# A Mamba block and an expert feed-forward layer on one core: statistics of x moved to ScalarE, one product of B and u moved from GpSimd to VectorE

## What is computed

```
x = x + mamba(layernorm(x))          # and inside it: rmsnorm, x @ W_in -> xs, res
    xs = silu(conv4(xs) + conv_b)    # 512 channels
    dt = softplus((xs @ W_x)[:, :512] @ W_dt);  B, C = 16 columns each of xs @ W_x
    h_t = exp(-exp(A_log) * dt_t) * h_(t-1) + dt_t * B_t * xs_t    # 512 channels x 16 states
    y_t = sum over the 16 states of h_t * C_t;   out = (y * silu(res)) @ W_out + residual
x = x + (silu(n @ w1[e]) * (n @ w3[e])) @ w2[e],  n = layernorm(x)   # expert e for tokens 512 e .. 512 e + 511
```

## Time and profile before

| | |
|---|---|
| median of three runs | 983.43 us |
| the profiled execution, its own time | 983.61 us |
| its span, first to last instruction | 981.8 us |
| TensorE matmul busy | 915.7 us (93%) |
| VectorE busy | 899.1 us (92%) |
| GpSimd busy | 891.0 us (91%) |
| ScalarE busy | 733.2 us (75%) |
| granted TensorE clock, mean | 0.979 |

### The profile page before, as it was taken

The page is one execution under the profiler, slowest core; times in us unless marked ns, Lnnn a source line. Parts: engine busy times, 40 slices in busy tenths (PEclk is TensorE's granted clock), DMA queues, the critical chain, the costliest instruction groups (busy, mean ns, idle before and its releaser), DMA issues.

```text
span 981.8 us, 13018 instructions
## 1 busy us (share of the span) xinstructions
PE 915.7 (93%) x4172; PEld 598.0 (61%) x4172; DVE 899.1 (92%) x966; ACT 733.2 (75%) x1305; POOL 891.0 (91%) x425
## 2 busy tenths in 40 slices
PE   6989989999999999999999999999999997869898
PEld 4555455655766566755756557755766566745765
DVE  5889899899999999999999999999999989999951
ACT  4577877988779878888779888888779785567630
POOL 1498899999999999999999999999999999999920
PEclk9998999999999999999999999999999999679899
DMA  5580144012742049021561038220480027200110
GB/s 175 212 308 22 43 185 204 4 65 65 268 186 67 2 148 353 18 68 59 212 247 43 25 103 326 89 68 21 176 320 16 31 99 284 92 21 4 59 50 21
DMA packets 43476, 116.82 MB, mean 119 GB/s; under 512 B 8592, under 2 KB 27024, under 8 KB 34192
## 3 DMA queue, kind: packets, MB, share of 16 engines
q1 hardware_dynamic: 41552, 115.94, 32.0%
q10 hardware_dynamic: 1856, 0.04, 0.1%
HBM read 110.21 MB, written 5.77 MB: 118 GB/s over the span
## 4 chain that ended last, share of the span: by engine, by line
PE 44%; DVE 20%; issue 14%; ACT 11%; POOL 10%; DMA 1%; DVEq 0%; POOLq 0%; SPq 0%; ACTq 0%
PE gbank L1095 18%; DVE ring L658 13%; PE gbank L1109 12%; PE ybank L1158 9%; POOL hc L516 7%; DVE ring L643 4%; ACT ebank L787 2%; POOL ring L502 2%; ACT hb L1022 2%; ACT sres L872 1%; DVE hb L738 1%; PE gbank L1103 1%; ACT L1027 1%; ACT L1020 1%; DMA hb<-in_L_attn_W_x_dram 1%
## 5 line engine op out<-in xcount | busy, mean ns | idle before, releaser
L658 DVE TENSOR_TENSOR_SCAN ring<-ebank,state,ring 128x512 f32<-128x512 f32 x512 | 623.2, 1268 | 31.1 <-ACT ebank L787 24.1
L516 POOL TENSOR_TENSOR hc<-ring,c_all 128x1024 f32<-128x1024 f32 x255 | 598.5, 2368 | 12.8 <-PE ybank L1158 6.9
L787 ACT ACTIVATE ebank<-dt_,a_neg 128x512 f32<-128x512 f32 x512 | 348.0, 688 | 149.6 <-DVE ring L658 145.8
L1158 PEld LDWEIGHTS ybank<-ident,hc 128*128 128x128 f32 x2048 | 239.1, 144 | 107.3 <-issue 54.9
L1158 PE MATMUL ybank<-ident,hc 128*128 128x128 f32 x2048 | 266.0, 279 | 33.2 <-POOL hc L516 19.2
L502 POOL TENSOR_TENSOR ring<-b_all,u 128x1024 f32<-128x1024 f32 x109 | 258.1, 2368 | 9.9 <-DVE taken L607 9.5
L643 DVE TENSOR_TENSOR ring<-b_all,ubank 128x1024 f32<-128x1024 f32 x145 | 173.5, 1196 | 0.0
L1095 PE MATMUL gbank<-xT,w 128*128 128x512 f32 x320 | 147.9, 597 | 9.8 <-DVE hb L738 8.5
L1095 PE MATMUL gbank<-xT,w_a 128*128 128x512 f32 x256 | 119.7, 604 | 8.0 <-DVE dt_ L632 4.4
L1095 PEld LDWEIGHTS gbank<-xT,w 128*128 128x128 f32 x320 | 57.3, 190 | 76.5 <-issue 56.7
L1095 PE MATMUL gbank<-xs,w_a 128*128 128x512 f32 x224 | 100.8, 593 | 0.7 <-ACT sres L805 0.7
(11 more groups left out here) (146 smaller groups left out, 749.4 us busy)
## 6 DMA issues: line engine op xcount, KB each, us to landing
b_all<-bc_kept SPq DMA_DIRECT2D x32, 1024.0 KB, 6.6
c_all<-bc_kept SPq DMA_DIRECT2D x32, 1024.0 KB, 8.4
w<-in_L_ffn_w_dram SPq DMA_DIRECT2D x16, 640.0 KB, 4.9
w_a<-in_L_attn_W_in_dram SPq DMA_DIRECT2D x7, 1024.0 KB, 5.0
w_a<-wc_kept SPq DMA_DIRECT2D x7, 1024.0 KB, 4.9
w2s<-in_L_ffn_w_dram SPq DMA_DIRECT2D x8, 640.0 KB, 9.3
xin<-in_L_attn_x_dram SPq DMA_DIRECT2D x9, 512.0 KB, 3.6
x<-in_L_attn_x_dram SPq DMA_DIRECT2D x7, 512.0 KB, 6.5
```

Source lines behind the costliest of these rows:

```text
L516: ch_ok.by(e.tensor_tensor(hc[:, q % HC, :, :], ring[:, q % RING, :, :], c_all[:, n:n + NG, :], ALU.mult))
L658: h_ok.by(e.tensor_tensor_scan(row, ebank[j % 2][:, :], row, initial=state[:, q, n:n + 1], op0=ALU.mult, op1=ALU.add))
L787: e_ok.by(e.activation(ebank[j % 2][:, :], dt_[:, d, :], ACT.Exp, scale=a_neg[:, d, k:k + 1]))
L1158: last = e.matmul(ybank[:, cols(b)], hc[:, q % HC, n, cols(b)], ident[:, :], is_transpose=True, start=(k == 0 and n == 0 and b == 0), stop ...
```

## The change

- The statistics of x for chunks 2 to 7 leave VectorE. ScalarE makes them instead: `x_sums` are four Copy activations of 128x256 whose accumulator output is the sum of a row, `x_mean` is one small activation, and `x_squares` are four Square activations with the negated mean as bias, again with accumulators. Their full results go to blocks 0 and 1 of `u` and are never used. `rooted` divides by 256 within its scale, and loses one small Copy.
- In iterations 1 to 5 they stand behind tiles 17, 21, 22 and 23 on ScalarE, and `rooted` moves from tile 22 to 26. GpSimd's `front` moves from tile 21 to 26, behind u's first block. GpSimd's products u of blocks 0 and 1 wait for the statistics, since these write there.
- The product of B and u of tile 21 goes from GpSimd to VectorE, where it stands behind `hidden` and `gated(1)`; `gated(1)` moves behind tile 20's `hidden` jobs.
- `residual(0, 1)` behind tile 5 becomes `residual(0)` behind tile 4 and `residual(1)` behind tile 5.
- Iteration 0 has its own places (tiles 23 to 26).

The diff, cut to its core:

```diff
-    POOL_BU = (1, 4, 7, 10, 11, 14, 17, 18, 21, 22, 23, 24, 27, 29)
+    POOL_BU = (1, 4, 7, 10, 11, 14, 17, 18, 22, 23, 24, 27, 29)
+    BEHIND = 21
+        sums = Event("sums", NT)
 # GpSimd, u_of
                     xs_ok.wait(e, c)
+                    if d < 2 and 1 <= c < E - 1:
+                        stats.wait(e, c + 1)
                     ub_ok.wait(e, c - 1, d + 1)
-            table = [(4, "scan", u_of(ND - 1)), (10, "back", back), (21, "next", front), (24, "front", u_of(0)),
+            table = [(4, "scan", u_of(ND - 1)), (10, "back", back), (24, "front", u_of(0)), (26, "next", front),
-            table0 = [..., (23, "next", front),
+            table0 = [..., (26, "next", front),
 # VectorE
+            def bu_behind(c, i):
+                bu(c, BEHIND)
-                if q + 1 < Q and q + 1 in dve_bu(c):
+                if q + 1 < Q and q + 1 in dve_bu(c) and (c == 0 or q + 1 != BEHIND):
-                     (19, "next", x_stats), (19, "scan", gated(1)), (20, "back", hidden(0)), (20, "back", hidden(1)),
-                     (20, "back", hidden_tail), (21, "back", hidden(2)), (22, "back", hidden(3)), (23, "back", hidden(4)),
+                     (20, "back", hidden(0)), (20, "back", hidden(1)),
+                     (20, "back", hidden_tail), (20, "scan", gated(1)), (20, "scan", bu_behind), (21, "back", hidden(2)), ...
-                      (19, "next", x_stats), (19, "scan", gated(0)), ...
+                      (19, "scan", gated(0)), ...
 # ScalarE
+            def x_sums(*bs):
+                def job(c, i):
+                    x_in.wait(e, c)
+                    bup_ok.wait(e, i, before(pool_bu(i), 2 * GPD))
+                    for b in bs:
+                        sums.by(e.activation(u[:, b // 2, b % 2 * D:(b % 2 + 1) * D], xin[:, b, :], ACT.Copy, accum_out=mv[:, b, 0:1]))
+                return job
+
+            def x_mean(c, i):
+                sums.wait(e, c - 2)
+                x1a_ok.wait(e, c - 3)
+                roots.by(e.activation(st[:, c % 3, 2, :], mv[:, :, 0], ACT.Copy, scale=-1.0 / D))
+
+            def x_squares(*bs):
+                def job(c, i):
+                    roots.wait(e, c, 1)
+                    for b in bs:
+                        last = e.activation(u[:, b // 2, b % 2 * D:(b % 2 + 1) * D], xin[:, b, :], ACT.Square, bias=st[:, c % 3, 2, b:b + 1], accum_out=mv[:, b, 1:2])
+                    if NT - 1 in bs:
+                        stats.by(last)
+                return job
 # ScalarE's table: removed (5, residual(0, 1)) and (22, rooted); added
+ (4, "back", residual(0)), (5, "back", residual(1)), (17, "next", x_sums(0, 1)), (21, "next", x_sums(2, 3)),
+ (21, "next", x_mean), (22, "next", x_squares(0, 1)), (23, "next", x_squares(2, 3)), (26, "next", rooted)
 # and its table0: (25, rooted) becomes
+ (23, "next", x_sums(0, 1)), (24, "next", x_sums(2, 3)), (25, "next", x_mean), (25, "next", x_squares(0, 1)),
+ (26, "next", x_squares(2, 3)), (26, "next", rooted)
```

More of the change, by code:

```diff
@@ L532, in _ @@
                     bu(0, q)
-            table = [(4, "scan", u_of(ND - 1)), (10, "back", back), (21, "next", front), (24, "front", u_of(0)),
+            table = [(4, "scan", u_of(ND - 1)), (10, "back", back), (24, "front", u_of(0)), (26, "next", front),
                      (27, "front", u_of(1)), (29, "front", u_of(2))]
-            table0 = [(3, "late", u_of(1)), (7, "late", u_of(2)), (10, "late", u_of(3)), (23, "next", front),
+            table0 = [(3, "late", u_of(1)), (7, "late", u_of(2)), (10, "late", u_of(3)), (26, "next", front),
                       (27, "front", u_of(0)), (28, "front", u_of(1)), (29, "front", u_of(2))]
@@ L757, in _ @@
             table = [(4, "back", gated(ND - 1)), (8, "back", m_stats), (12, "scan", gated(0)), (17, "front", dt_of(0)),
-                     (19, "next", x_stats), (19, "scan", gated(1)), (20, "back", hidden(0)), (20, "back", hidden(1)),
-                     (20, "back", hidden_tail), (21, "back", hidden(2)), (22, "back", hidden(3)), (23, "back", hidden(4)),
+                     (20, "back", hidden(0)), (20, "back", hidden(1)),
+                     (20, "back", hidden_tail), (20, "scan", gated(1)), (20, "scan", bu_behind), (21, "back", hidden(2)), (22, "back", hidden(3)), (23, "back", hidden(4)),
                      (26, "front", dt_of(1)), (27, "front", dt_of(2)), (28, "ahead y", gated(2)), (30, "scan y", gated(2)),
@@ L762, in _ @@
             table0 = [(0, "late", fed), (4, "late", dt_of(1)), (5, "late", dt_of(2)), (9, "late", dt_of(3)),
-                      (19, "next", x_stats), (19, "scan", gated(0)), (23, "scan", gated(1)), (27, "front", dt_of(0)),
+                      (19, "scan", gated(0)), (23, "scan", gated(1)), (27, "front", dt_of(0)),
                       (27, "front", dt_of(1)), (29, "front", dt_of(2)), (30, "scan", gated(2)), (30, "front", dt_of(ND - 1))]
@@ L812, in rooted @@
                 mine, eps, eps2 = st[:, c % 3, :, :], consts[:, 0, 0:1], consts[:, 1, 0:1]
[L813 to L816, removed]
+                of = 1.0 if c < 2 else 1.0 / D
+                roots.by(e.activation(mine[:, 0, :], mv[:, :, 1], ACT.Ln, scale=(1.0 + EPS) * of, bias=eps2))
+                roots.by(e.activation(mine[:, 1, :], mv[:, :, 1], ACT.Ln, scale=of, bias=eps))
+                if c < 2:
+                    roots.by(e.activation(mine[:, 2, :], mv[:, :, 0], ACT.Copy, scale=-1.0))
+                roots.wait(e, c, 3)
                 roots.by(e.activation(mine[:, 4:8:3, :], mine[:, 0:2, :], ACT.Exp, scale=-0.5))
@@ L1067, in _ @@
             table = [(0, "front", before_conv(0)), (1, "front", before_conv(1)), (2, "front", before_conv(2)), (2, "back", y_read(ND - 1)),
-                     (3, "front", before_conv(3)), (3, "front", convolved(0)), (4, "front", convolved(1)), (5, "front", convolved(2)), (5, "back", residual(0, 1)),
+                     (3, "front", before_conv(3)), (3, "front", convolved(0)), (4, "front", convolved(1)), (4, "back", residual(0)), (5, "front", convolved(2)), (5, "back", residual(1)),
                      (7, "front", convolved(3)), (8, "front", silus), (9, "back", rooted2), (9, "back", m_copy),
                      (10, "scan", y_read(0)), (11, "front", res(0, 1)), (12, "back", normal2), (13, "front", res(2, 3)),
-                     (13, "front", bc_read), (14, "back", turned("OXT")), (16, "front", softplus(0)), (17, "back", gate(0, 1)),
+                     (13, "front", bc_read), (14, "back", turned("OXT")), (16, "front", softplus(0)), (17, "back", gate(0, 1)), (17, "next", x_sums(0, 1)),
                      (18, "back", gate(2, 3)), (18, "scan", y_read(1)), (19, "back", gate(4)), (19, "back", tails),
-                     (20, "back", gate_silus), (22, "next", rooted), (24, "front", softplus(1)), (25, "front", softplus(2)),
+                     (20, "back", gate_silus), (21, "next", x_sums(2, 3)), (21, "next", x_mean), (22, "next", x_squares(0, 1)),
+                     (23, "next", x_squares(2, 3)), (24, "front", softplus(1)), (25, "front", softplus(2)), (26, "next", rooted),
                      (26, "ahead y", y_read(2)), (27, "scan y", y_read(2)), (28, "next", normal_rows(0, 1)), (29, "next", normal_rows(2, 3)), (30, "front", softplus(ND - 1)),
@@ L1083, in _ @@
                       (18, "front", convolved(1)), (18, "front", convolved(2)), (19, "front", convolved(3)),
-                      (19, "front", silus_first), (20, "scan", y_read(1)), (20, "front", res(0, 1)), (22, "front", res(2, 3)),
-                      (24, "front", bc_read), (25, "next", rooted), (25, "front", softplus(0)), (27, "front", softplus(1)),
+                      (19, "front", silus_first), (20, "scan", y_read(1)), (20, "front", res(0, 1)), (22, "front", res(2, 3)), (23, "next", x_sums(0, 1)),
+                      (24, "front", bc_read), (24, "next", x_sums(2, 3)), (25, "next", x_mean), (25, "next", x_squares(0, 1)), (26, "next", x_squares(2, 3)),
+                      (26, "next", rooted), (25, "front", softplus(0)), (27, "front", softplus(1)),
                       (27, "scan", y_read(2)), (28, "next", normal), (29, "front", softplus(2)), (30, "front", softplus(ND - 1)),
```

## The result

The changed kernel takes 986.23 us (median of 9 runs, 984.98 to 987.84). The kernel before took 983.77 us in the same session (9 runs, 982.61 to 984.33). The ratio is 1.0028, 95% interval 1.0019 to 1.0037. The profiled execution of the changed kernel took 985.15 us, with a span of 983.4 and a mean granted clock of 0.983; the one before took 983.61, with 981.8 and 0.979.

The account below looks back on a forecast made before the run. Two loops, VectorE's and TensorE's, meeting in ScalarE's block 0.42 us apart, were taken as the bound, not GpSimd. Terms 2.6 + 0.5 - 0.6 - 0.4 = +2.1 us on 983.61 gave 985.7, stated as 985.6; range 979.5 to 990.

Parts of the forecast that it names:

- x_stats leaving: VectorE beside ScalarE's block before scan 21: removing about 2 us of statistics gains 0, since scan 21 waits for its decay.
- Tile 21's product: Costs VectorE 0 in the hole x_stats leaves; GpSimd's 2.3 us relief gains 0 in iterations 1 to 6, waiting for scan 21.
- residual's split: ScalarE at tile 5: tile 6's decays start earlier, taking 0.70 us off VectorE's loop, 0.75 in iteration 1.
- front behind tile 26: `scales` comes at about 481.5, behind tile 29's product; ScalarE waits 2.7 us and VectorE 1.3 before scan 29.
- x_sums: ScalarE behind tile 17: a pair costs 0.87 us, 0.43 of it covered, so scan 18 stalls 0.45 (bounds 0.2 and 0.9).
- Rival D: Accumulators on ScalarE are dear, from about 1.5 us a pair; at 1.7 us, 990 us in all; chance 0.15.
- The slack: Before scan 21: VectorE was ready 0.42 us before tile 20's second decay, so its loop is that much shorter.
- VectorE's loop: Through tile 19's last scan and tile 20's second decay to scan 21: later by 1.05 less 0.42, 0.65 us a period.
- TensorE's 0.5: Share of scan 29's 1.3 us stall reaching TensorE through the xT copies: 0.5 us a period, between 0 and 1.3.
- A: Rival: GpSimd is the bound after all, 2.33 us go in six periods and once in the last iteration: 967 us; chance 0.12.
- B: Rival: the new wait for `scales` is covered and VectorE's loop falls by up to 0.42 in five periods: 980.3 us; chance 0.10.
- C: Rival: nothing is moved, stalls hide in one another as TensorE's path sets the pace: 983.4 us (982.4 to 984.8); chance 0.18.

Follow-up runs that it names:

- Experiment 8: Kernel before with only ScalarE's read of y of block 2 moved from tile 27 to 26: 982.21 us, period 112.37.
- experiment 5: Changed kernel with GpSimd's `front` at tile 27 instead of 26, one product later: 1000.93 us, period 115.6 to 116.1.
- Experiment 3: Changed kernel with x statistics back on VectorE at tile 19, `rooted` at 22, `front` at 21 (iteration 0 keeps 26): 982.65 us, period 112.35.
- experiment 1: Changed kernel with GpSimd's `front` at tile 25 instead of 26, before tile 29's product: 982.27 us, period 112.36.
- experiments 2: Changed kernel with tile 21's product of B and u given back to GpSimd: 986.38 us, period 113.27.
- experiment 10: Kernel before with y read at tile 26 and GpSimd's tile 21 product of B and u halved in chunks 1 to 7: 981.63 us, period 112.37.
- experiment 11: Kernel before with y read at tile 26 and GpSimd's tile 24 product of B and u halved in chunks 1 to 7: 978.81 us, period 112.00.
- experiment 7: Changed kernel with `front` at tile 25, first sums at tile 15, all four residual blocks back at tile 5: 982.87 us, period 112.53.
- experiment 12: Changed kernel with statistics on VectorE, `rooted` 22, `front` 21, y read at 26, u's first block on VectorE at tile 20: 983.93 us, period 112.74.
- experiments 6: Changed kernel with `front` at tile 25, first sums at tile 15 and y read at tile 26: 982.89 us, period 112.34.
- 9: Changed kernel with `front` at 25, first sums at 15, y read at 26, GpSimd's tile 24 product halved in chunks 1 to 7: 978.82 us, period 111.89.

## Why the prediction was right, point by point

**The time.** Predicted 985.6, measured 986.23; the sum was +2.1 us on the profiled execution, which grew by 1.54, while the medians differ by 2.46. Term by term, from the Silus of the two traces: up to iteration 1 the changed kernel gains 2.10 us (0.6 predicted), the four periods from iteration 1 to 5 lose 3.27 (2.6), the one to iteration 6 loses 0.75 (0.5), the one to iteration 7 nothing (0), and the end gains 0.4 (0.4). Of the first term about 1.5 us are not the change's: its first scan starts 0.50 us earlier, and at scan 12 of iteration 0 it gains 1.03 more. Experiment 8, which is the kernel before but for one edit far behind that point, gains 0.43 and the same 1.03 there, and experiment 5, the changed kernel but for `front`, gains neither. Of the second, 0.34 are the excess of iteration 3. Without these two the traces give about +2.7, so each of the two loss terms was given somewhat too low, and differences between executions hid part of that. One execution differs from another by 1 to 1.5 us here, and more than the sign and the order of the sum should not be read from one pair of traces.

**x_stats leaving: 0.** Right. Experiment 3 puts them back without a measurable difference to experiment 1 (112.35 and 112.36, which another loop holds).

**Tile 21's product: 0 on VectorE, 0 from GpSimd's relief.** Right in iterations 1 to 6: the hole was there (0.83 us of wait remain) and GpSimd waits 2.44 us at tile 21, where 2.3 or more were foreseen. Experiments 2 and 10 show it as cause. By the Trainium skill's rule (Perfetto Trace Analysis, Identifying the Most-Contended Engine) the relief of the engine with the highest occupancy comes first; experiment 11 shows the rule's point only for a stretch, the one behind scan 21, and experiment 10 shows it empty 12 us earlier on the same engine. In the last iteration the cost was not 0. ScalarE's block ahead of scan 21 is shorter there, and scan 20 gains 0.48 us while scan 21 loses 1.62, a net 1.14 that the prediction did not have. The wait for a GpSimd product at tile 24 went with it (-0.86), as foreseen, and the part from the last Silu to the end came out 0.4 us shorter, as given.

**residual's split: -0.70.** Measured -0.66 at scan 6, and -0.72 in iteration 1, where -0.75 was given. That is the saving on VectorE's path; experiment 7 shows that with `front` in time only 0.18 of it reaches the period.

**front behind tile 26.** `scales` at 481.2 (predicted 481.5), ScalarE's wait 2.57 us (2.7), VectorE's 1.15 (1.3), the step at scan 29 +1.23. Experiments 1 and 5 show that this wait makes the slowdown.

**x_sums: 0.87 a pair, stall 0.45.** Measured 0.80 and 0.39. Rival D is out: a sum with its read takes 0.40 us, not 0.85.

**The slack: 0.42.** Measured 0.27: scans 20 and 21 together move by -2.57 + 2.30. In the kernel before, scan 19 ends at 559.54 (the next product starts 0.08 us before that end, so its start was the wrong mark) and the second decay starts at 559.85.

**Which loop ruled.** I gave VectorE's loop 0.65 and TensorE's 0.5, and let VectorE's rule in the first four of the five periods. The traces bear this out. The chain that ended last, by engine, from the pages of the kernel before and of the changed one:

```profile
PE 44%; DVE 20%; issue 14%; ACT 11%; POOL 10%; DMA 1%; DVEq 0%; POOLq 0%; SPq 0%; ACTq 0%
```

```profile
DVE 42%; issue 19%; ACT 16%; PE 13%; POOL 9%; DMA 1%; DVEq 0%; POOLq 0%; SPq 0%; ACTq 0%
```

The last step ahead of the Silu block is the second decay of tile 20. In the kernel before it starts 0.61 us after the first, and scan 19 has ended 0.31 us earlier, so VectorE does not hold it. In the changed kernel it starts 0.72 us after the first (1.08 in iteration 3), and 0.03 to 0.04 us after the end of scan 19, in each of iterations 1 to 5. In iteration 3 the wait is long enough for the timeline of ScalarE to print it; below it, the chain of iteration 5, which comes from VectorE and through the sums:

```profile
447.00 0.69 ACT L794 ACTIVATE ebank<-dt_,a_neg 128x512 f32<-128x512 f32 x1 [0.40 <-DVE ring L665]
```

```profile
665.83 0.90 ACT u L819 x4
...
672.25 1.27 DVE ring L665
...
673.54 0.69 ACT ebank L794
```

So the wait for `scales` and the stall at scan 18 both count there: 0.73 a period against the 0.65 given. That ScalarE still waits 1.11 us for TensorE's TAIL (559.04) does not speak against it, since a second wait comes behind that one.

**The term that was mis-sized: TensorE's 0.5.** It was a choice between bounds of 0 and 1.3, with no row between. ScalarE takes TAIL 109.80 us after the last Silu (559.04 - 449.24), against 109.22 in the kernel before (558.75 - 449.53, in ScalarE's timeline there):

```profile
558.75 0.59 ACT L1017 ACTIVATE hb<-gbank 64x512 f32<-64x512 f32 x1 [1.12 <-PE gbank L1095]
```

That is 0.58 us in the steady iterations. In iteration 6, where the sums are gone, TensorE's path is last, as predicted, but the period grew by 0.75 and not by 0.5. The way by which TensorE receives the delay was wrong too. I had the copies of xT behind `normal_rows`; the chain of iteration 6 comes along VectorE's scans from scan 29 up to tile 17, and only there turns to TensorE, through ScalarE's copies of the gate:

```profile
777.65 0.69 ACT ebank L794
778.34 1.01 ACT hb L812 x2
...
779.39 1.98 PE gbank L1128 x4
...
785.72 0.02 ACT hb L1048
...
786.22 1.29 ACT ebank L794 x2
```

The first of these gate copies starts 0.59 us later after the last Silu than in the kernel before in steady iterations (102.35 against 101.76), and 0.74 us later in iteration 6, the same as TAIL. So the two loops are one up to tile 17: TensorE gets the 1.23 us of scan 29 less the 0.66 us of scan 6, that is 0.57, and in iteration 6 0.13 us more, which VectorE loses at scan 14 for a cause that I did not follow. That 0.5 was near is luck. No experiment moves the gate copies, so this way is read from the chain and from equal shifts, not shown by a run.

**The rivals.** A (967) is refuted by experiments 2 and 10. B's condition, `scales` in time, was not met, but experiment 1 makes it true and shows B's price: 982.3, not 980.3, since GpSimd's stretch behind scan 21 holds 112.35, where B had 112.1, and the part from the last Silu to the end took 84.3 us, 0.7 more than before (0.6 of it at scan 27, open). C is out with the ratio's interval.

## What to carry to other kernels

A result that another engine needs should stand in the queue ahead of the long instruction, not behind it: one slot of a small operation (0.2 us) on GpSimd, ahead of or behind a 2.35 us product, was worth 3 to 4 us here, and one more slot 15 us. Relief of a full engine is worth something only in the stretch in which nothing else ties it down, so look for its first wait behind the saved work before counting the saving; 0.3 us of waiting was enough here. Where several loops lie within half a microsecond, add each edit's time to all of them, also to that of the engine that takes the work over, and look where the loops run over the same instructions: a delay there counts in both.

## What the runs showed of the hardware

An activation with an accumulator is two instructions of ScalarE. The groups of the changed kernel's trace by line and shape (count, busy us in all, mean ns):

```profile
L831 ACT ACTIVATE u<-xin,st 128x256 f32<-128x256 f32 x24 | 11.8, 494 | 0.0
...
L819 ACT ACTIVATE u<-xin 128x256 f32<-128x256 f32 x24 | 9.7, 406 | 0.0
...
L819 ACT ACTIVATION_READ_ACCUMULATOR u<-xin 128x1 f32 x24 | 4.6, 192 | 0.0
```

The read takes 0.19 us, of which 0.09 lie ahead of the next instruction's start (553.25 to 553.34). The lengths of the copy and of the square agree with the Trainium skill (ScalarE: Activation LUTs, What ACT_TABLE_LOAD costs): 186 ns + 0.833 x 256 is an estimate of 399 ns, and 93 ns more for the bias by pointer make 492. The read comes on top of these.

A product of two operands in SBUF took VectorE very different times: 0.69 us for 128x512 with no GpSimd instruction running, and 1.16 to 1.60 us beside a GpSimd product of B and u (experiment 12). GpSimd takes 1.27 us for the same. No run isolates the cause.

The other surprise is the 1.03 us between executions at scan 12 of iteration 0. It goes with the granted TensorE clock of the stretch from 62 to 112 us. Five of the fourteen traces have 0.97 there (the changed kernel and experiments 6, 8, 9 and 11), and in all five scan 12 gains 1.03 to 1.05 us on the kernel before; the other nine have 0.93, and their steps lie between -0.48 and +0.13. The times show it too: in the later sessions the kernel before took 983.52 to 984.45 us in its 31 runs with a mean clock of 0.979, and 981.99 to 982.62 in its 25 runs with 0.983. The changed kernel took 984.98 to 986.46 in five runs with 0.983, and 987.29 and 987.84 in two with 0.979. At a mean clock of 0.983 the means differ by 3.3 us (985.63 and 982.36, in different sessions), more than the 2.46 of the medians. Clock and time go together here, but no run was made to test which causes which, and the mean clock does not order the runs of every kernel: experiment 8 took 981.17 to 981.57 at 0.979 and 983.29 and 983.34 at 0.981.
